# Maxima per source in a graph kernel: blank blocks first, segment maxima of early columns during the scatter

## The reference, cut to what matters

```python
e = beta[0] * edge_weight
seg_max = jax.ops.segment_max(e, src, num_segments=n)
ex = jnp.exp(e - seg_max[src])
seg_sum = jax.ops.segment_sum(ex, src, num_segments=n)
p = ex / seg_sum[src]
msg = norm_h[src] * p[:, None]
h = jax.ops.segment_sum(msg, dst, num_segments=n)
```

## Time and profile before

| | |
|---|---|
| median of 3 runs | 6702.77 us (6701.74 to 6705.58) |
| profiled execution, its own time | 6699.18 us |
| its span | 6697.7 us |
| PE busy | 4445.1 us (66%) |
| DVE busy | 3983.5 us (59%) |
| ACT busy | 1573.7 us (23%) |
| POOL busy | 1564.2 us (23%) |
| share of the clock granted to PE | 0.856 |

### The profile page before, as it was taken

The page is one execution under the profiler, slowest core; times in us unless marked ns, Lnnn a source line. Parts: engine busy times, 40 slices in busy tenths (PEclk is TensorE's granted clock), DMA queues, the critical chain, the costliest instruction groups (busy, mean ns, idle before and its releaser), DMA issues. The chain is left out here.

```text
span 6697.7 us, 52624 instructions
## 1 busy us (share of the span) xinstructions
PE 4445.1 (66%) x15996; PEld 2524.8 (38%) x15998; DVE 3983.5 (59%) x4400; ACT 1573.7 (23%) x1840; POOL 1564.2 (23%) x1634
## 2 busy tenths in 40 slices
PE   3501111337999999898888888788879887444443
PEld 1100000024554454687333378433334443333333
DVE  6412122678887786698999979899990111111112
ACT  0000000001579700444455410255540003000000
POOL 1677777100000000000000000000000001777776
PEclk9999999999999999656999965799999998555555
DMA  3001010143468606354333346333326666222222
GB/s 58 6 10 18 10 16 12 27 174 134 121 171 237 184 1 246 98 166 125 115 111 111 115 138 188 101 115 111 112 95 245 245 245 172 52 53 53 53 53 56
DMA packets 624187, 729.35 MB, mean 109 GB/s; under 512 B 96339, under 2 KB 556401, under 8 KB 604703
## 3 DMA queue, kind: packets, MB, share of 16 engines
q1 hardware_dynamic: 571790, 669.98, 32.4%
q0 software_dynamic: 52144, 56.00, 3.5%
HBM read 542.42 MB, written 183.38 MB: 108 GB/s over the span
## 5 line engine op out<-in xcount | busy, mean ns | idle before, releaser
L1080 POOL DMA_INDIRECT ring<-rel_dram,rel_pair x806 | 765.6, 950 | 4709.5 <-POOLq L68 4464.2
L878 PE MATMUL total<-to,from 128*128 128x384 f32 x2816 | 939.4, 492 | 34.3 <-issue 28.5
L1625 PE MATMUL sums<-acc,hw 128*64 128x392 f32 x2144 | 747.5, 504 | 138.0 <-DVE acc L1559 137.6
L1160 PE MATMUL total<-ring,onehot 128*128 128x128 f32 x1612 | 415.3, 439 | 579.0 <-DMA ring<-rel_dram,rel_pair 578.5
L517 POOL DMA_INDIRECT cells_dram<-rec,place x742 | 715.8, 965 | 226.1 <-issue 220.0
L686 PE MATMUL alike<-right,left 18*128 18x512 bf16 x352 | 174.4, 616 | 818.6 <-DVE top L646 662.3
L878 PEld LDWEIGHTS total<-to,from 128*128 128x128 f32 x2816 | 524.0, 190 | 450.0 <-issue 121.7
L1115 DVE TENSOR_SCALAR onehot<-iota,loc_pair 128x128 f32<-128x128 f32 x806 | 179.9, 286 | 814.8 <-PE total L1160 814.8
L1160 PEld LDWEIGHTS total<-ring,onehot 128*128 128x128 f32 x1612 | 357.2, 324 | 636.9 <-issue 636.8
L1625 PEld LDWEIGHTS sums<-acc,hw 128*64 128x64 f32 x2144 | 269.7, 138 | 581.2 <-issue 306.9
L620 DVE CAST lo_i<-rows 128x128 int32<-128x128 f32 x11 | 2.7, 244 | 714.8 <-DMA rows<-cells_dram 714.8
(11 more groups left out here) (341 smaller groups left out, 5977.6 us busy)
## 6 DMA issues: line engine op xcount, KB each, us to landing
strip<-ac_dram SPq DMA_DIRECT2D x100, 1600.0 KB, 6.5
count<-ac_dram SPq DMA_DIRECT2D x200, 784.0 KB, 4.2
ac_dram<-stage SPq DMA_DIRECT2D x625, 192.0 KB, 2.4
lo_row<-lo_dram SPq DMA_DIRECT2D x44, 1024.0 KB, 7.3
h<-ac_dram SPq DMA_DIRECT2D x26, 1600.0 KB, 8.3
acc<-ac_dram SPq DMA_DIRECT2D x24, 1600.0 KB, 8.8
rel_dram<-rows SPq DMA_DIRECT2D x25, 1024.0 KB, 5.4
mask_dram<-mask SPq DMA_DIRECT2D x25, 800.0 KB, 5.6
```

Source lines behind the costliest of these rows:

```text
L878: nc.tensor.matmul(spots[:, at(spot), 0:WIDTH].rearrange("p o n -> p (o n)"), from_[:, n % RING, u, :], to[:, n % RING, u, :, :].rearrange ...
L1080: pool.indirect_dma_start(ring[:, j % SLOTS, :], None, m.rel_dram[:, :], bass.IndirectOffsetOnAxis(ap=m.rel_pair[:, j:j + 1], axis=0)).the ...
L1160: last = nc.tensor.matmul(total[:, at(col, D)], onehot[:, j % U, :], ring[:, j % SLOTS, :], start=False, stop=False, skip_group_check=True)
L1625: last = nc.tensor.matmul(psum[kk * 2 * HC:(kk + 1) * 2 * HC, banks(i) + q, 0:PIECE], hw[:, t, k, :], p[n % 3][:, piece], start=t == 0, st ...
```

## The change

`source_tops` takes the blocks in the order 9, 10, 0 to 8 instead of 0 to 10: n counts the steps, b is the block. Buffers, semaphores and PSUM go by n, columns by b. One more small DMA reads the last number of `ends_dram` (chunks in use); DVE subtracts 4096 from the groups needed of each block that begins at or beyond it (a blank block), so that it waits for one group only. The blocks of the last two steps (7 and 8) both wait for all groups, and their rows are loaded and prepared together. The columns are now in three ranges: blocks 0 to 6, blocks 7 and 8, blocks 9 and 10. The segment maxima of the first and the third range are made ahead of step 9's `prep`, those of blocks 7 and 8 at the end. The lines left out rename b to n for buffers and semaphores in `prep`, on ACT and on PE.

```diff
-    RANGES = [(0, (KB - 1) * P), ((KB - 1) * P, NCH)]
+    RANGES = [(0, (KB - 4) * P), ((KB - 4) * P, (KB - 2) * P), ((KB - 2) * P, NCH)]
+    ORDER = [KB - 2, KB - 1, *range(KB - 2)]
...
-        seg, seg_row, of_tile = sb("seg", [P, 2, NT]), sb("seg_row", [NT, P]), sb("of_tile", [NT, NCH])
+        seg, seg_row, of_tile = sb("seg", [P, 3, NT]), sb("seg_row", [NT, P]), sb("of_tile", [NT, NCH])
...
+        used_i, used, first, blank = sb("used_i", [KB, 1], I32), sb("used", [KB, 1]), sb("first", [KB, 1]), sb("blank", [KB, 1])
...
+            sp.dma_start(used_i[:, :], m.ends_dram[NCELLS - 1:NCELLS].rearrange("(o j) -> o j", o=1).to_broadcast([KB, 1])).then_inc(tables_in, 16)
...
-            for b in range(KB):
-                if b < KB - 1:
+            def rows_of(n):
+
+                b = ORDER[n]
+                if n >= 2:
+                    sp.wait_ge(prepped, n - 1)
+                    sp.wait_ge(turned, n - 1)
+                sp.dma_start(rows[:, n % 2, :, :], m.cells_dram[b * BLOCK_EDGES:(b + 1) * BLOCK_EDGES, :].rearrange("(k e) c -> k e c", e=P)
+                             ).then_inc(rows_in[n % 2], 16)
+
+            for n, b in enumerate(ORDER):
+                if n < KB - 2:
                     groups_needed = sp.value_load(until_row[0:1, b:b + 1], min_val=1, max_val=len(SORTED))
                     sp.wait_ge(landed, groups_needed)
                     sp.nop(nofuse=True)
-                else:
+                    rows_of(n)
+                elif n == KB - 2:
                     sp.wait_ge(landed, len(SORTED))
-                if b >= 2:
-                    sp.wait_ge(prepped, b - 1)
-                    sp.wait_ge(turned, b - 1)
+                    rows_of(n)
+                    rows_of(n + 1)
+                sp.wait_ge(prepped, n + 1)
                 edges = slice(b * BLOCK_EDGES, (b + 1) * BLOCK_EDGES)
-                sp.dma_start(rows[:, b % 2, :, :], m.cells_dram[edges, :].rearrange("(k e) c -> k e c", e=P)).then_inc(rows_in[b % 2], 16)
-                sp.wait_ge(prepped, b + 1)
-                sp.dma_start(m.edge_rows_dram[:, edges].rearrange("n (k e) -> k n e", e=P), planes[:, b % 2, :, :]).then_inc(stored, 16)
-                sp.dma_start(m.lo_dram[edges].rearrange("(k e) -> k e", e=P), lo_b[:, b % 2, :]).then_inc(stored, 16)
-                sp.wait_ge(stored, 32 * (b + 1))
-                for q in range(b * PARTS, (b + 1) * PARTS):
+                sp.dma_start(m.edge_rows_dram[:, edges].rearrange("n (k e) -> k n e", e=P), planes[:, n % 2, :, :]).then_inc(stored, 16)
+                sp.dma_start(m.lo_dram[edges].rearrange("(k e) -> k e", e=P), lo_b[:, n % 2, :]).then_inc(stored, 16)
+                sp.wait_ge(stored, 32 * (n + 1))
+                for r in range(PARTS):
+                    q = n * PARTS + r
                     if q >= 2:
                         sp.wait_ge(laid, per_part * (q - 1))
-                    cols = slice(q * PART * P, (q + 1) * PART * P)
+                    cols = slice((b * PARTS + r) * PART * P, (b * PARTS + r + 1) * PART * P)
                     sp.dma_start(right[q % 2][:, :], m.edge_rows_dram[:, cols]).then_inc(part_in[q % 2], 16)
...
-            dve.wait_ge(tables_in, 32)
+            dve.wait_ge(tables_in, 48)
             step(v.tensor_copy(tile_all[:, :], tile_all_i[:, :]))
             step(v.tensor_scalar(below[:, :], tile_all[:, :], last_tile[:, 0:1], None, ALU.is_le, ALU.add, accum_out=until[:, :]))
             step(v.tensor_scalar(until[:, :], until[:, :], float(NPAIRS), float(G - 1 - HEAD), ALU.min, ALU.add))
+            step(v.tensor_copy(used[:, :], used_i[:, :]))
+            step(v.tensor_scalar(first[:, :], m.pcol[0:KB, :], float(P), None, ALU.mult))
+            step(v.tensor_tensor(blank[:, :], used[:, :], first[:, :], ALU.is_le))
+            step(v.scalar_tensor_tensor(until[:, :], blank[:, :], -4096.0, until[:, :], ALU.mult, ALU.add))
...
             prep(0)
-            for b in range(KB):
-                if b == KB - 1:
+            for n, b in enumerate(ORDER):
+                if n == KB - 2:
                     tops_of(0)
-                    prep(b)
-                for i in range(b * P // 8, (b + 1) * P // 8):
-                    if i == b * P // 8 + 12 and b + 1 < KB - 1:
-                        prep(b + 1)
+                    tops_of(2)
+                    step(v.tensor_tensor(seg[:, 0, :], seg[:, 0, :], seg[:, 2, :], ALU.max))
+                    prep(n)
+                    prep(n + 1)
+                for k in range(P // 8):
+                    i, c0 = n * P // 8 + k, b * P + k * 8
+                    if k == 12 and n + 1 < KB - 2:
+                        prep(n + 1)
                     dve.wait_ge(laid, i + 1)
-                    v.tensor_reduce(top[:, i * 8:(i + 1) * 8], psum[:, i % 3, :, :], AX.X, ALU.max).then_inc(peaked, 1)
-                dve.wait_ge(peaked, (b + 1) * P // 8)
+                    v.tensor_reduce(top[:, c0:c0 + 8], psum[:, i % 3, :, :], AX.X, ALU.max).then_inc(peaked, 1)
+                dve.wait_ge(peaked, (n + 1) * P // 8)
```

More of the change, by code:

```diff
@@ L613, in _, with prep @@
             step(v.tensor_scalar(of_tile[:, :], tile_row[0:NT, :], m.pcol[0:NT, 0:1], None, ALU.is_equal))
[L615 to L620, removed]
+            def prep(n):
+                dve.wait_ge(rows_in[n % 2], 16 * (n // 2 + 1))
+                if n >= 2:
+                    dve.wait_ge(stored, 32 * (n - 1))
+                step(v.tensor_copy(lo_i[:, :], rows[:, n % 2, :, 0]))
                 step(v.tensor_tensor(shifted[:, :, :], mid(lo_i[:, :], BITS), shifts[:, :, :], ALU.arith_shift_right))
                 step(v.tensor_scalar(shifted[:, :, :], shifted[:, :, :], 1, None, ALU.bitwise_and))
[L623 to L627, removed]
+                step(v.tensor_copy(planes[:, n % 2, 3:3 + BITS, :], shifted[:, :, :]))
+                step(v.tensor_scalar(planes[:, n % 2, 3 + BITS:, :], shifted[:, 0:BITS - 1, :], -1.0, 1.0, ALU.mult, ALU.add))
+                step(v.tensor_copy(lo_b[:, n % 2, :], lo_i[:, :]))
+                step(v.tensor_scalar(ev[:, :], rows[:, n % 2, :, 2], m.beta[:, 0:1], None, ALU.mult))
+                split3(dve, step, v, ev[:, :], [planes[:, n % 2, k, :] for k in range(3)], rest[:, :], back[:, :])
                 v.nop().then_inc(prepped, 1)
@@ L659, in _ @@
         def _(act):
-            for b in range(KB):
-                act.wait_ge(turned, b + 1)
+            for n, b in enumerate(ORDER):
+                act.wait_ge(turned, n + 1)
                 cols = slice(b * P, (b + 1) * P)
-                nc.scalar.activation(m.ends_col[:, :, cols], tp[:, b % 2, 0:2 * P].rearrange("p (c e) -> p c e", c=2), ACT.Copy)
-                nc.scalar.activation(m.w_col[:, cols], tp[:, b % 2, 2 * P:3 * P], ACT.Copy).then_inc(copied, 1)
+                nc.scalar.activation(m.ends_col[:, :, cols], tp[:, n % 2, 0:2 * P].rearrange("p (c e) -> p c e", c=2), ACT.Copy)
+                nc.scalar.activation(m.w_col[:, cols], tp[:, n % 2, 2 * P:3 * P], ACT.Copy).then_inc(copied, 1)
         @block.tensor
@@ L670, in _ @@
             pe.wait_ge(coded, 2)
[L671 to L674, removed]
+            for n in range(KB):
+                pe.wait_ge(rows_in[n % 2], 16 * (n // 2 + 1))
+                if n >= 2:
+                    pe.wait_ge(copied, n - 1)
                 for c in range(3):
-                    last = nc.tensor.transpose(tp[:, b % 2, c * P:(c + 1) * P], rows[:, b % 2, :, c], m.ident[:, :])
+                    last = nc.tensor.transpose(tp[:, n % 2, c * P:(c + 1) * P], rows[:, n % 2, :, c], m.ident[:, :])
                 last.then_inc(turned, 1)
-                for q in range(b * PARTS, (b + 1) * PARTS):
+                for q in range(n * PARTS, (n + 1) * PARTS):
                     pe.wait_ge(part_in[q % 2], 16 * (q // 2 + 1))
```

## The result

The changed kernel takes 6588.08 us (median of 4 runs, 6583.62 to 6591.26) against 6702.26 us before (median of 4, 6696.57 to 6705.58): ratio 0.983, 95% interval 0.9816 to 0.9844. That is 114 us less; 109.5 were forecast, and 6593 us lay 5 us beside the median. On another chip the pair was 6577.85 and 6694.34 us (0.9829, 0.9815 to 0.9842).

What follows compares the result with a forecast made beforehand. The prediction took POOL's scatter, then DVE's tail, as the bounds. The tail's 128.5 us gain less 19.0 us of longer scatter gave 109.5 us, so 6589.7, or 6593 us as median; range 6574 to 6621.

Steps and rivals of the forecast that it cites:

- The tail: From block 7's `prep` to the last segment maximum: 72.1 us instead of 200.6, 128.5 us less.
- T': Moment when `prep` of block 7 begins in the changed kernel, after the scatter; forecast at 1226.0 us.
- The cover: Beside the scatter: blank blocks hidden from about 270 to 340 us, early maxima ending at 1211.1 us.
- Two more `prep`: Beside the scatter: two further `prep` lengthen POOL's indirect DMAs by 0.7 us each, 1.4 us.
- `tops_of(0)`: Early maxima over 896 columns beside the scatter: 45.0 us of DVE work, costing the scatter 13.4 us.
- The beat: Under early maxima over 896 columns, POOL passes one indirect DMA per 1.80 us round instead of each 1.263 us.
- `tops_of(2)`: Early maxima over 256 columns beside the scatter: one DMA each two rounds, 4.2 us lost.
- the second claim: Some 0.7 us after its start, an indirect DMA again waits for a holding DVE instruction to end.
- the clock's rival: Later stages meet the lower clock level differently: 10 to 20 us more or less; chance 0.05.
- No contention: Early maxima don't hold POOL's DMAs: 14.9 us better than forecast, 6578 us; chance 0.12.
- heavier contention: Early maxima hold POOL longer, or both engines wait fully for each other: 6620 or up to 6641 us; chance 0.12.
- the flag: Blank flag fails, so all eleven blocks lie behind the scatter: some 209 us more, about 6910; chance 0.03.

Runs made afterwards that it cites:

- e1: Changed kernel's block order with blank blocks first, but all segment maxima at the end; 6614.28 us, ratio to the kernel before 0.9879.
- e3: e1 with 50 more tensor_scalar over 896 columns beside the scatter; single run, line 517 in sum 2.7 us longer than in e1.
- e4: e1 with 50 more tensor_tensor_reduce (two inputs) over 896 columns beside the scatter; single run, indirect DMAs 731.9 us in sum against 717.0 in e1.
- the ten profiles: Profiles of the kernel before, the changed kernel (two) and seven experiments, all with the same scatter code.
- the second profile: The changed kernel unaltered, measured again on another chip beside e6; 6577.85 us.
- e6: Changed kernel with the hidden segment maxima cut into ranges of at most 256 columns and spread over the scatter; 6565.89 us against 6577.85.
- e5: e1 with 50 more tensor_reduce (one input) over 896 columns beside the scatter; single run, indirect DMAs 717.2 us in sum, as in e1.

## Why the prediction was right

- **The tail.** T' + 15.7, + 33.9, + 52.1, + 72.1 stood at 15.6, 33.8, 52.0 and 71.9. SP's second reload (1254.75) came in time. Both loads together landed 0.8 us later than one (1223.78 to 1227.31 against 2.7 us).
- **The cover.** Blank blocks from 278 us, done before block 0's rows at 391; early maxima done 10.4 us before T'. With e1's scatter and load (949.0 us from the first DMA to block 7's `prep`) they would have ended 2.4 us too late, some 3 forecast; the stretch covered them.
- **Two more `prep`.** 1.4 us forecast, 1.2 measured (e1).
- **`tops_of(0)`.** The beat of one DMA a round held to 0.01 us: 13.4 us forecast, 12.7 measured (0.40 and 23 times 0.535). The agreement is in part luck. The forecast said that line 634 alone suffices for the beat and that it matters little whether line 635 holds too. The runs show the opposite: each DMA of the beat is held by line 651 (635 before), 50 tensor_scalars of this width cost 1.8 us in e3, and 50 of the others 14 in e4. Stepping through the two queues by the rules of the last section, with line 650 alone holding, gives 2 to 3 us for `tops_of(0)` (an estimate; no run has it), which would have put T' some 10 us earlier than forecast.
- **`tops_of(2)`: the mis-sized term.** 4.2 us forecast, 1.0 measured (five DMAs of 1.15 us). The step that failed is the second claim of the earlier trace rows as the forecast used it: that it waits for whatever line 634 or 635 is under way. Line 651 doesn't hold it (in e4 the same instruction ran across all but the first 0.04 us of the DMA at 1171.70), and line 650 over 256 columns is over in 0.29 us, too short to meet both ends of it (last section). What the earlier trace rows showed was not wrong: the DMA at 538.67 ends 0.84 us after line 621 and 0.11 after line 622, a tensor_scalar, and so do all 60 DMAs of the ten profiles that met this line of `prep`, about 0.01 us later than nearly all that met others. That fits a second claim that waits for the tensor_scalar, and costs this hundredth only. So the scatter grew by 14.0 (15.4 in the second profile), not 19.0.
- **The rest.** The 5 us less in the scatter, with the later start of that profile against it, put line 669 at 1299.2 where 1298 was forecast. The stages behind kept their lengths within 4 us (from the first hot row, lines 730 and 750, to the end 5265.8 before and 5261.8 after), and the granted clock its mean (0.856 to 0.854): the clock's rival did not show.
- **The rivals.** No contention fell with the beat; heavier contention with the DMAs that pass beside a busy DVE; the flag held.

## What to carry to other kernels

Work moved beside a queue of indirect DMAs is free only in DVE's time: ask, instruction by instruction, whether it has two SBUF inputs or is a tensor_scalar or cast, and what round the two queues fall into. Where they are periodic, the loss is a beat and hangs on the width: 896 columns cost three tenths of POOL's rate (1.26 to 1.80 us), 256 columns a twentieth (five rounds of 0.79 for three DMAs). And when blocks come in order of readiness, those that are ready from the start belong first, if something in the data tells which they are.

## What the runs showed of the hardware

Two rules give the end of each of the 7420 indirect DMAs of line 517 in the ten profiles within 0.03 us; the first alone misses 17 of them, by 0.07 to 0.29 us. The first was put to the test by e3 to e6; the second was read off the same traces afterwards, and no run was made for it.

First: a DVE instruction with two SBUF inputs, a tensor_scalar or a cast between SBUF tiles that has been under way for over 0.05 us when an indirect DMA starts, and lasts over 0.13 us more, puts the DMA's end 0.83 us after its own, whatever its length (0.43 us in `tops_of(2)`, 3.48 in the earlier trace rows). A tensor_reduce doesn't (e5), nor does the one tensor_scalar that also writes a sum (line 616, 1.13 us long, 0.39 us under way at the DMA of 270.84 us in the changed kernel, which took 0.96).

Second: a tensor_scalar or cast that is under way 0.50 us after the DMA's start and is still under way 0.83 us after it puts the DMA's end 0.12 us after its own. Of the 17, this one is from the kernel before; line 613 began 0.14 us after the DMA's start:
```profile
266.58 1.21 POOL L517 DMA_INDIRECT cells_dram<-rec,place  x1 [0.30 <-issue]
266.72 0.94 DVE L613 TENSOR_SCALAR of_tile<-tile_row,pcol 25x1408 f32<-25x1408 f32 x1 [0.47 <-DMA tile_row<-cell_dram]
```
An instruction with two SBUF inputs in the same place does nothing (e4, 1171.70).

And the turn goes by who is first: a tensor_scalar or cast that begins between 0.51 and 0.69 us after the start of a DMA that nothing holds is itself longer, by 0.07 to 0.24 us, as if it had begun 0.70 to 0.77 us after it (107 such in the ten profiles; line 650 at 1151.81 us is one). Two-input instructions that began there kept their length (16 such; line 651 over 896 columns took its 1.09 us). So each side waits for a part of the other's instruction, DVE by a quarter of a microsecond at most. Which step of the DMA stands behind either claim, no run shows.
